# The attention programs of TensorE and ScalarE written out for eight batches

## What is computed

```
x = x + xattn(layernorm(x), ctx)      # 16 heads of 32, causal, keys and values from a latent of 128
x = x + ffn(layernorm(x))             # 8 experts

xattn: q = h @ Wq.T ; k, v = split(ctx @ Wkv.T)
       attn = softmax(mask(q k^T / sqrt(32))) ; out = (attn v) @ Wout.T
ffn:   logits[t, o, e] = h @ router_w.T + router_b ; probs = softmax over e
       w, sel = top_k(probs, 2), normalised ; c[t, e] = sum over o of the weights
       final = sum over e of c[t, e] * (h @ expert_w[e].T + expert_b[e])
```

## Time and profile before

| | us |
|---|---|
| median of 3 runs | 1986.51 |
| the 3 runs | 1984.96, 1986.51, 1989.05 |
| span of the profiled execution, first to last instruction | 1984.3 |
| PE busy in it | 1910.6 (96%) |
| VectorE, ScalarE, GpSimd busy | 1432.1, 1039.0, 850.5 |

### The profile page before, as it was taken

One profiled execution on the slowest core, in us unless ns is written; L12 is line 12 of the kernel. 1 busy time (PEld: TensorE's weight loads), 2 busy tenths in 40 slices (PEclk: granted clock), 3 DMA queues, 4 the chain that ended last, 5 costly groups with the idle time before them and its releaser, 6 DMA issues.

```text
span 1984.3 us, 30426 instructions
## 1 busy us (share of the span) xinstructions
PE 1910.6 (96%) x9772; PEld 1514.7 (76%) x9772; DVE 1432.1 (72%) x2840; ACT 1039.0 (52%) x2062; POOL 850.5 (43%) x1016
## 2 busy tenths in 40 slices
PE   4899999999998999999999999999999999999999
PEld 3666766777765788888888888778888888888887
DVE  5667667767668658787888888477777777777732
ACT  2566566566554347877777787533443333344400
POOL 5577777777674135456445435102321111232100
PEclk8999999999999999999999999999999999999999
DMA  5454555455466468787856555822232222223111
GB/s 166 121 125 130 137 144 128 124 149 134 108 166 229 159 229 274 231 271 221 254 203 217 190 186 196 313 85 79 94 118 85 80 95 85 80 86 124 49 42 33
DMA packets 103693, 294.54 MB, mean 148 GB/s; under 512 B 13777, under 2 KB 14801, under 8 KB 98482
## 3 DMA queue, kind: packets, MB, share of 16 engines
q1 hardware_dynamic: 91394, 209.44, 33.1%
q10 hardware_dynamic: 8880, 67.37, 10.5%
q0 software_dynamic: 3328, 16.78, 3.7%
HBM read 150.31 MB, written 109.16 MB: 131 GB/s over the span
## 4 chain that ended last, share of the span: by engine, by line
PE 83%; DVE 7%; DMA 3%; issue 2%; POOL 2%; ACT 2%; ACTq 0%; SPq 0%; DVEq 0%; POOLq 0%
PE pair L261 20%; PE pair L263 20%; PE pair L262 20%; PE pair L672 3%; PE ps L721 3%; PE ps L261 3%; PE pair L705 3%; PE ps L262 3%; PE ps L263 3%; DMA w_raw<-w_fix 1%; DVE pair L1390 1%; PE ps L741 1%; DVE w_raw L1525 1%; POOL pT L1836 1%; PE ps L902 1%
## 5 line engine op out<-in xcount | busy, mean ns | idle before, releaser
L261 PE MATMUL pair<-w_h,hT 128*128 128x512 f32 x1920 | 751.7, 392 | 6.4 <-ACT w_h L1201 3.6
L263 PE MATMUL pair<-w_h,hT 128*128 128x512 f32 x1920 | 748.5, 390 | 0.0
L262 PE MATMUL pair<-w_l,hT 128*128 128x512 f32 x1920 | 748.3, 390 | 0.0
L1908 POOL TENSOR_TENSOR logits<-logits,second 128x512 f32<-128x512 f32 x224 | 298.6, 1370 | 590.9 <-DVE second L1605 590.6
L261 PEld LDWEIGHTS pair<-w_h,hT 128*128 128x128 f32 x1920 | 361.4, 188 | 81.9 <-issue 5.8
L263 PEld LDWEIGHTS pair<-w_h,hT 128*128 128x128 f32 x1920 | 361.1, 188 | 75.8
L262 PEld LDWEIGHTS pair<-w_l,hT 128*128 128x128 f32 x1920 | 361.3, 188 | 74.1
L1708 DVE SCALAR_TENSOR_TENSOR xb<-pair,c_all,xb 128x512 f32<-128x512 f32 x256 | 191.7, 749 | 195.6 <-PE pair L263 189.5
L1095 ACT ACTIVATE pT<-pair,zero 128x1024 f32<-128x1024 f32 (+3 forms) x256 | 202.6, 792 | 192.0 <-PE pair L705 183.6
L1390 DVE CUSTOM_DVE_ANT_0 pair<-pair,future 128x256 f32<-128x256 f32 (+3 forms) x340 | 184.1, 554 | 124.3 <-PE pair L672 115.9
L1191 ACT ACTIVATE w<-tree 128x512 f32<-128x512 f32 x32 | 20.3, 635 | 388.6 <-DVE tree L1607 388.6
(11 more groups left out here) (166 smaller groups left out, 2609.7 us busy)
## 6 DMA issues: line engine op xcount, KB each, us to landing
logits<-lg_all ACTq DMA_DIRECT2D x32, 1792.0 KB, 8.9
qk_st<-qk SPq DMA_DIRECT2D x372, 128.0 KB, 2.4
lg_all<-ev_a SPq DMA_DIRECT2D x31, 768.0 KB, 8.5
lg_all<-ev_b SPq DMA_DIRECT2D x31, 768.0 KB, 3.8
xb<-x SPq DMA_DIRECT2D x64, 256.0 KB, 2.9
hT_all<-hT SPq DMA_DIRECT2D x32, 512.0 KB, 4.3
hT<-hT_all SPq DMA_DIRECT2D x32, 512.0 KB, 4.0
xt<-in_x SPq DMA_DIRECT2D x8, 1024.0 KB, 5.4
```

What stands on the lines that cost most here:

```text
L261: pe.matmul(dst, lh, rh, start=start, stop=False)
L262: pe.matmul(dst, lh, rl, start=False, stop=False)
L263: return pe.matmul(dst, ll, rh, start=False, stop=stop)
L1908: pool.tensor_tensor(logits[t % 2][:, e - 1, :], logits[t % 2][:, e - 1, :], second[:], ALU.subtract)\
```

## The change

In `over_batches` the register loop goes. `body` is called for all eight batches with `b` as a Python number, and with the same three flags as before. Values of waits are then constants in the instructions. Nothing else is touched; lines below the edit have numbers smaller by 3.

```diff
         def over_batches(eng, body, epilogue):
 
-            body(0, True, True, True)
-            with eng.Fori(1, B - 2) as b:
-                body(b, False, True, True)
-            body(B - 2, False, True, False)
-            body(B - 1, False, False, False)
+            for b in range(B):
+                body(b, b == 0, b < B - 1, b < B - 2)
             epilogue()
```

## The result

The changed kernel is slower. In 12 runs its median is 1991.71 us (1987.89 to 1993.21), that of the kernel before in 12 runs 1986.31 (1983.26 to 1991.75); the ratio is 1.0025, 95% interval 1.0017 to 1.0032. By the ratio that is +5.0 us (by the medians +5.4) where -3.4 was forecast, and 1991.71 lies outside the range. The profiled execution took 1989.64 us with a span of 1987.9.

What follows compares the result with a forecast made beforehand. PE's matmul distances were taken to bound the kernel. Registers and branch together save 0.68 us per batch, 3.4 over five, longer programs add nothing: 1986.51 - 3.4 = 1983.1 us, range 1980.6 to 1986.8.

Steps and rivals of the forecast that it cites:

- What bounds the kernel: Whole kernel: PE busy 1910.6 of 1984.3 us; only shorter distances between its matmuls help; the loop holds 363.60 us.
- Register instructions: Attention batches 1 to 5, PE and ACT: removal gains 0.68 us per batch, 3.4 in all, bounds 1.85 and 3.6.
- The branch: Loop's back edge on PE: worth about 0.11 us, 4 of them, already inside the per-batch gain and not added.
- Longer programs: Code fetch in attention: some 16 more q8 packets, 0.28 MB, cost already in batch 6's 72.02 us, nothing added.
- what hides it: PE's code fetch in attention: a packet is needed every 18 us and takes 1.44 us, so it is covered.
- the prediction's own signs: Router or expert stretch changing by more than 1 us, or a clock falling elsewhere, would make the prediction wrong.
- Rival E: Attention: PE's code arrives late, 16 packets each by 1.44 us, 23 us slower, 2009.5; 4% with other code stalls.
- What follows waits for PE, so the gain arrives undiminished: Router and experts: untouched, keep their lengths and begin 3.4 us earlier, so attention's gain reaches the end.
- Rivals B, C and D: B: nothing arrives, 1986.5, 10%; C: ACT gains more, 1981.5, 9%; D: back edge costs a fetch, 1977.3, 2%.

Runs made afterwards that it cites:

- pad80: Changed kernel with 80 more instructions, waits that already hold, at the head of PE's program: 1985.27 us, 0.9991 of the kernel before.
- the later transfers: Kernel before, with POOL issuing each 1 MB transfer into w_fix only once the router's next token block has landed: 1985.27 us, 0.9994.
- the three kernels named above: Against the kernel before: ACT's program alone written out, 0.9995; changed kernel with 80 instructions at PE's head, 0.9991; the latter with earlier nm_h copy, 0.9997.

## Why the prediction was wrong, point by point

**What bounds the kernel**: right. PE's distances are the time, and the loop's share was measured rightly.

**Register instructions**: 0.68 us per batch was forecast and 0.74 measured in pad80, where no packet fell on the row copies (mean of the first four batches 72.00 against 72.74). Taking the upper bound was right, and the reason given for it too: PE's wait for the exponentials fell from 1.5 to 0.7 us.

**The branch**: 0.12 us at the one edge that can be read against the earlier trace rows (0.28 in place of 0.40). Right.

**Longer programs** is the step that failed, in the words "I add nothing for it". It counted the packets rightly (16 more) and priced them at nothing, since batch 6 had four of them and was the shortest of all rows. But a packet's price depends on its place, and batch 6 before had its four at 9.0 to 12.8 us after L687. I took one sample of one placement for the cost of a packet in general, and "what hides it" asked only whether the code comes in time, never whom the packet keeps waiting. In the profiled execution batches 2 to 5 took 73.1, 73.1, 73.3 and 73.9 us instead of 72.0, some 5.3 us more, so batches 1 to 5 together came out 1.8 us longer than before and not 3.5 shorter.

The rest of the way in the two profiled executions: the changed kernel's router starts 6.1 us later than before. Beside the 1.8 us, 1.7 were lost ahead of batch 1, in a group of batch 0 with a granted clock of 0.90 in place of 1.00; the kernel before shows the same 0.90 there in its execution with the later transfers, whose attention is untouched, so this differs between executions and is not a cost of the change. Another 0.5 us were lost in batch 6 and 2.1 behind it, in part to the clock (0.50 from 577.8 to 581.0). Router and experts were 1.0 and 1.5 us shorter. That makes 3.6 us between the two spans, where all the runs give 5.0. By the prediction's own signs a clock that fell at another place and a stretch that changed by over 1 us spoke against it; neither explains the batches that got longer.

**Rival E** named the right queue and the right sign, and the wrong mechanism. From 120 to 500 us PE waits in the changed kernel for the same things as in pad80, for about the same times, and beside them only for nm_l (3.2 us in 6 waits); nothing shows a late program. And 1.44 us for each of 16 packets would have been 23 us. It had 4% because I never asked which DMA has no time to spare. No row of the prediction showed the landing of qk_st<-nm_l against its use (1.8 us against the 1.9 from its issue to L702); the view of DMA issues had the first.

**"What follows waits for PE, so the gain arrives undiminished"**: wrong too, though the changed kernel's own router was not the victim. In the three kernels named above, whose attention got faster, the router took 3 to 5 us more, through a load issued 0.45 us or more behind a 1 MB transfer. **Rivals B, C and D**: no sign of any. In pad80 the batches take 72.0 us with full work, not 72.7 as B has it, and they never went under 71.9.

**Open**: why the packets stay near the row copies once they are there (batches 3 to 6). PE's program waits for the same nm_l (L730 in the order) as SP does for its copy, and in those batches 15 of 16 packets of q8 start 0.3 to 4.3 us after nm_l is ready; that PE runs on from there at once and so asks for code at that moment is argued, not shown. Open too is why the late packet's semaphore event comes 1.1 us after its record, and why SP's issue of nm_l takes twice as long when a q8 packet has started just ahead of it (the three cases above).

## What to carry to other kernels

Code is traffic. Here writing a loop out put fetches at places that the length of the program sets, and a transfer that landed just in time met them. Before unrolling, look in the trace for DMAs with little time between landing and use (0.1 us here, where a packet cost up to 1), and give those time first. If a version with more or fewer idle instructions at its head differs by several us, the placement is what is being measured. And a gain of a few us in one stage has to be followed to the end, since transfers of the next can then meet differently.

## What the runs showed of the hardware

PE held a loop of one whole batch without fetching it again: in the kernel before, q8 brought 4 packets between 132 and 182 us, in the loop's first pass, and was silent until 490 us. In each written-out batch but the last it brought some 4 packets of 16 KB, each some 0.9 to 1.8 us long by the records. A copy of 8 KB in 16 packets that met such a fetch landed up to 2 us late, mostly by a single one of its packets. The waits that stand at register instructions in the loop cost 0.72 to 0.74 us per batch of 72.7, on PE and ACT together.
